# Two fp32 attention layers on one core: 96-row stacks of high and low halves replaced by plain fp32 matmuls on 16-row heads

## What is computed

```
x = x + attention0(layernorm(x), ctx)    # weights W + 2 A B (rank 16), biases
x = x + sqrt((n @ cos(..))**2 + (n @ sin(..))**2),  n = layernorm(x)
x = x + attention1(layernorm(x), ctx)    # q and k are rotated (rope), biases
x = x + quantised feed-forward(layernorm(x)), 256 -> 1024 -> 256
```

## Time and profile before

| | |
|---|---|
| three runs | 2496.88, 2500.81, 2504.37 us; median 2500.81 |
| profiled execution, first to last instruction | 2491.9 us |
| first attention: first to last exponential | 110.6 to 843.6 us |
| second attention: first to last exponential | 1079.7 to 2083.9 us |
| busy over the span: PE, DVE, ACT, POOL | 78%, 70%, 53%, 32% |

### The profile page before, as it was taken

One profiled execution on the slowest core, in us unless ns is written; L12 is line 12 of the kernel. 1 busy time (PEld: TensorE's weight loads), 2 busy tenths in 40 slices (PEclk: granted clock), 3 DMA queues, 4 the chain that ended last, 5 costly groups with the idle time before them and its releaser, 6 DMA issues. The chain is left out here.

```text
span 2491.9 us, 47293 instructions
## 1 busy us (share of the span) xinstructions
PE 1955.9 (78%) x14240; PEld 1576.1 (63%) x14240; DVE 1747.3 (70%) x3674; ACT 1316.8 (53%) x2381; POOL 797.0 (32%) x866
## 2 busy tenths in 40 slices
PE   1689999999999679277788777887777775786687
PEld 0567777777777467255666666666666663665676
DVE  6567778877877378465667767767666665676788
ACT  0255666656655378144444444444444443786676
POOL 3012222222222200423333333333333332221787
PEclk9899999999999689578888888888888877898899
DMA  5576887888878100356665656666666661356565
GB/s 164 107 157 145 169 172 162 166 169 166 170 161 165 53 3 0 76 104 122 123 120 116 117 109 116 119 112 118 111 118 122 121 118 54 135 220 252 196 242 186
DMA packets 259781, 333.54 MB, mean 134 GB/s; under 512 B 29152, under 2 KB 237184, under 8 KB 251520
## 3 DMA queue, kind: packets, MB, share of 16 engines
q1 hardware_dynamic: 233088, 277.00, 49.4%
q0 software_dynamic: 26624, 55.67, 9.6%
HBM read 185.70 MB, written 144.70 MB: 133 GB/s over the span
## 5 line engine op out<-in xcount | busy, mean ns | idle before, releaser
L610 DVE TENSOR_REDUCE L_negm<-L_s_bank 128x2 f32<-128x512 f32 x1024 | 684.4, 684 | 363.2 <-PE L_s_bank L418 360.7
L475 ACT ACTIVATE L_prob<-L_t_bank 128x512 f32<-128x512 f32 x1024 | 598.9, 598 | 631.8 <-PE L_t_bank L429 625.7
L418 PE MATMUL L_s_bank<-L_kst,L_qst 96*128 96x256 f32 x2048 | 526.1, 343 | 236.5 <-DMA L_kst<-k_scratch 176.7
L418 PEld LDWEIGHTS L_s_bank<-L_kst,L_qst 96*128 96x128 f32 x2048 | 355.4, 216 | 363.0 <-issue 142.0
L429 PE MATMUL L_t_bank<-L_qst,L_kst 98*128 98x256 f32 x2048 | 460.6, 311 | 18.3 <-ACT L_prob L475 15.2
L429 PEld LDWEIGHTS L_t_bank<-L_qst,L_kst 98*128 98x128 f32 x2048 | 361.7, 217 | 33.3 <-ACT L_prob L475 30.0
L339 PE MATMUL L_o_bank<-L_prob,L_vext 128*32 128x256 f32 x4096 | 301.1, 415 | 2.7 <-ACT L_prob L475 2.7
L1289 PE MATMUL G_acc<-G_w_out,G_hhl 128*128 128x256 f32 x1024 | 140.4, 291 | 59.4 <-DVE G_hhl L1259 59.1
L259 POOL DMA_DIRECT2D L_den<-o_scratch x64 | 35.5, 554 | 452.2 <-DMA o_scratch<-L_osb 452.2
L1289 PEld LDWEIGHTS G_acc<-G_w_out,G_hhl 128*128 128x128 f32 x1024 | 127.9, 192 | 72.1 <-DVE G_hhl L1259 37.5
L339 PEld LDWEIGHTS L_o_bank<-L_prob,L_vext 128*32 128x32 f32 x4096 | 112.5, 115 | 92.6 <-issue 18.8
(11 more groups left out here) (172 smaller groups left out, 3257.2 us busy)
## 6 DMA issues: line engine op xcount, KB each, us to landing
L_qst<-q_scratch SPq DMA_DIRECT2D x384, 128.0 KB, 5.0
L_kst<-k_scratch SPq DMA_DIRECT2D x384, 128.0 KB, 6.4
q_scratch<-L_qhl SPq DMA_DIRECT2D x64, 512.0 KB, 3.0
k_scratch<-L_khl SPq DMA_DIRECT2D x64, 512.0 KB, 3.2
o_scratch<-L_osb POOLq DMA_DIRECT2D x128, 256.0 KB, 4.8
hidden_scratch<-G_hid SPq DMA_DIRECT2D x32, 1024.0 KB, 3.9
G_hid<-hidden_scratch SPq DMA_DIRECT2D x32, 1024.0 KB, 7.4
L_ctx_in<-in_ctx SPq DMA_DIRECT2D x64, 256.0 KB, 3.2
```

The lines of the kernel that those rows point to most:

```text
L418: mm = pe.matmul(s_bank[k % 2][:, j, :], qst[1 - q][0:96, h, P * qt:P * (qt + 1)], kst[1 - q][0:96, h, :], start=True, stop=True)
L475: act.activation(prob[g % 2][:, k % 2, 2 * (k // 2 % 2):2 * (k // 2 % 2) + 2, :], t_bank[k % 2][:, :, :], ACT.Exp, scale=HD ** -0.5).then_ ...
L610: dve.tensor_reduce(negm[:, t, 2 * pair:2 * pair + 2, qt], s_bank[k % 2][:, :, :], AX.X, ALU.max, negate=True).then_inc(sem["dve_s"], 1)
```

## The change

It touches `attention`, `start` and the constants; the two feed-forward layers stay. A row of the changed kernel names that kernel's own lines (there the scores are L307, the transposed scores L324).

- No halves. A projection is 4 plain fp32 matmuls. Layer 1 has two more weights, `qr` and `kr`, whose output is the rotated half, so that the shuffle and its multiplication go; POOL multiplies both parts with cos and sin at once (1024 elements a partition) and adds them (`rotate`), one q and one k a step.
- Heads lie where the projection puts them, 16 features in each 32-row strip of the array (`qs`, `ks`; the odd heads are copied to the strips' first rows by four transfers each, `odd_heads`). A score matmul contracts 16 rows, a transposed one 17; the 17th holds ones in `ks` and the negated maxima in `qs`. In a slot they are issued in turn, score and transposed score, in strips two apart.
- The weighted sums of a step are two blocks of 16 matmuls (`weighted`) and leave PSUM in one copy `eo` to `osb`. `den` is filled by SP from `osb`, `rden` goes straight to `rin`, two plain fp32 matmuls with `bsel` spread it (L413), VectorE multiplies. The odd heads' results are moved by four transfers (`merge`).
- ctx is transposed once and stored (`c_dram`), layer 1 reads it back. The bias of v goes into that of the output. Normalising x moves from ScalarE to POOL.
- All small transfers stand in SP's queue; POOL issues none. The loop over sequences is unrolled. `drive` makes steps -2 to 33.

```diff
-        qst = [sb(f"qst{j}", [98, H, S], F32R) for j in range(2)]
-        kst = [sb(f"kst{j}", [98, H, S], F32R) for j in range(2)]
-        prob = [sb(f"prob{j}", [P, NT, 4, S]) for j in range(2)]
-        vext = [sb(f"vext{j}", [P, NT, H, SLOT]) for j in range(2)]
-        whl = {n: sb(f"w{n}", [P, 2, KT, D], F32R) for n in "qkvo"}
-        ctx_in = sb("ctx_in", [P, NT, D])
+        NP = 4 if rope else 2
+        qs = [sb(f"qs{j}", [P, 2 * KT, S]) for j in range(3)]
+        ks = [sb(f"ks{j}", [P, 2 * KT, S]) for j in range(3)]
+        prob = [sb(f"prob{j}", [P, NT, 4, KT, S]) for j in range(2)]
...
-        yhl = xT
-        negm = sb("negm", [P, 2, HT, NT])
-        mhl = sb("mhl", [P, 2, 2, HT * NT], F32R)
-        mT = sb("mT", [2 * HT * NT, 2, P], F32R)
+        xT = sb("xT", [P, KT, S])
...
+        bvc = sb("bvc", [P, KT])
+        bvx = sb("bvx", [P, KT, P])
         bo = sb("bo", [P, D])
...
-            cos, sin = sb("cos", [P, S]), sb("sin", [P, S])
-            rr = sb("rr", [P, KT, S])
-        s_bank = [ps(f"s_bank{j}", [P, 2, S]) for j in range(2)]
...
+        t_bank = [ps(f"t_bank{j}", [P, KT, S]) for j in range(2)]
+        eo = ps("eo", [P, 2, KT, S])
+        m0, m1 = ps("m0", [P, KT, S]), ps("m1", [P, KT, S])
...
-        def drive(eng, step):
-
-            for i in range(-2, 5):
-                step(i, i % 2)
-            with eng.Fori(2, (B - 4) // 2) as r:
-                step(2 * r + 1, 1)
-                step(2 * r + 2, 0)
-            for i in range(B - 3, B + 3):
-                step(i, i % 2)
-
...
+        def drive(step):
+            for i in range(-2, B + 2):
+                step(i, i + 2 < B, 0 <= i + 1 < B, 0 <= i < B, 0 <= i - 1 < B, 0 <= i - 2)
...
-            def stack(dst, dram, order, t, done):
-                for c, part in enumerate(order):
-                    sp.dma_start(dst[HD * c:HD * (c + 1), HT * t:HT * (t + 1), :].bitcast(F32),
-                                 dram[part, t].rearrange("(h d) q -> d h q", d=HD)).then_inc(done, 16)
...
+            def odd_heads(buf, done):
+                for g in range(4):
+                    sp.dma_start(buf[32 * g:32 * g + HD, 2:4, :], buf[32 * g + HD:32 * g + 2 * HD, 0:2, :]).then_inc(done, 16)
+
+            def maxima(n, c):
+                sp.wait_ge(sem["dve_mT"], 2 * n + c + 1)
+                sp.dma_start(qs[n % 3][16:P:32, 2 * c:2 * c + 2, :], mT[c][:, :]).then_inc(sem[f"m_load{c}"], 16)
...
+                if d_on:
+                    sp.wait_ge(sem["act_eo"], i)
+                    after(sp, sem["dve_rd"], i - 1)
+                    for c in range(2):
+                        sp.dma_start(den[64 * c:64 * (c + 1), :], osb[(i - 1) % 2][HD - HD * c:P:32, c, :, :]).then_inc(sem["den_load"], 16)
                 if a_on:
...
+                    sp.wait_ge(k_ready, i + 3)
+                    odd_heads(ks[(i + 2) % 3], sem["odd_k"])
+                if d_on:
+                    sp.wait_ge(sem["den_load"], 32 * i)
+                    after(sp, sem["merge"], 64 * (i - 1))
+                    for g in range(4):
+                        sp.dma_start(osb[(i - 1) % 2][32 * g + HD:32 * g + 2 * HD, 0, :, :],
+                                     osb[(i - 1) % 2][32 * g + HD:32 * g + 2 * HD, 1, :, :]).then_inc(sem["merge"], 16)
+                if a_on:
+                    sp.wait_ge(q_ready, i + 3)
+                    odd_heads(qs[(i + 2) % 3], sem["odd_q"])
+                if d_on:
+                    sp.wait_ge(sem["dve_rd"], i)
+                    after(sp, sem["pe_r"], i - 1)
+                    sp.dma_start(rin[:, :], rden[:, :]).then_inc(sem["r_load"], 16)
                 if b_on:
-                    m_rows(i + 1, 1 - q, 0)
+                    maxima(i + 1, 0)
                 if a_on:
...
+                    sp.wait_ge(sem["odd_k"], 64 * (i + 3))
+                    after(sp, sem["ones"], 16 * (i + 2))
+                    sp.dma_start(ks[(i + 2) % 3][16:P:32, 0:2, :], ones[:, :, :]).then_inc(sem["ones"], 16)
+                    sp.wait_ge(sem["odd_q"], 64 * (i + 3))
...
+            def rotate(n, dst, parts, full, free, done, base):
+                pool.wait_ge(full, n + 1)
+                pool.tensor_tensor(parts[:, :, :, :], parts[:, :, :, :], cs[:, :, :].unsqueeze(2).to_broadcast([P, 2, KT, S]),
+                                   ALU.mult).then_inc(sem["pool_rope"], 1)
+                pool.wait_ge(sem["pool_rope"], base + 1)
+                pool.tensor_tensor(dst[:, 0:2, :], parts[:, 0, :, :], parts[:, 1, :, :], ALU.add).then_inc(done, 1)
...
-            def project(dst, wt, act):
-
+            def project(dst, weight, act):
                 for f in range(KT):
-                    group = [(k, cw, ca) for cw, ca in ((0, 0), (0, 1), (1, 0)) for k in range(KT)]
-                    for j, (k, cw, ca) in enumerate(group):
-                        mm = pe.matmul(dst[:, f, :], wt[:, cw, k, P * f:P * (f + 1)], act[:, ca, k, :],
-                                       start=j == 0, stop=j == len(group) - 1)
+                    for k in range(KT):
+                        mm = pe.matmul(dst[:, f, :], weight[:, k, P * f:P * (f + 1)], act[:, k, :], start=k == 0, stop=k == KT - 1)
                 return mm
...
+            def scores(n, k):
+                c, g, qt = k // 8, (k % 8 // 2 + 2) % 4, k % 2
+                if k == 0:
+                    pe.wait_ge(q_ready, n + 1)
...
+                after(pe, sem["dve_s"], 16 * n + k - 1)
+                rows = slice(32 * g, 32 * g + HD)
+                for t in range(KT):
+                    mm = pe.matmul(s_bank[k % 2][:, t, :], qs[n % 3][rows, 2 * c + t, P * qt:P * (qt + 1)], ks[n % 3][rows, 2 * c + t, :],
+                                   start=True, stop=True)
+                    if t == KT - 1:
+                        mm.then_inc(sem["pe_s"], 1)
+                    yield
...
+                after(pe, sem["act_p"], 16 * n + k - 1)
+                rows = slice(32 * g, 32 * g + HD + 1)
+                for t in range(KT):
+                    mm = pe.matmul(t_bank[k % 2][:, t, :], ks[n % 3][rows, 2 * c + t, P * kt:P * (kt + 1)], qs[n % 3][rows, 2 * c + t, :],
+                                   start=True, stop=True)
+                    if t == KT - 1:
+                        mm.then_inc(sem["pe_t"], 1)
+                    yield
...
+                        if a_on and not rope:
+                            pe.wait_ge(sem["ctx_load"], 16 * (n + 1))
+                            after(pe, sem["act_v"], n)
+                            after(pe, sem["dve_y"], i - 1)
...
+                    if k == xT_at and a_on:
+                        pe.wait_ge(sem["pool_xn"], n + 1)
+                        after(pe, sem["dve_mT"], 2 * i + 2)
+                        after(pe, sem["act_k"] if rope else sem["act_q"], n)
                         transposes(m0, xn).then_inc(sem["pe_xT"], 1)
...
+                    if k == o_at and e_on:
+                        pe.wait_ge(sem["dve_y"], i - 1)
+                        pe.wait_ge(sem["act_xT"], min(n + 1, B))
+                        after(pe, sem["dve_mT"], min(2 * i + 2, 2 * B))
+                        after(pe, sem["dve_x"], i - 2)
+                        project_rows(m0, yT, wt["o"]).then_inc(sem["pe_o"], 1)
+                    if k == q_at and a_on:
+                        pe.wait_ge(sem["act_xT"], n + 1)
+                        after(pe, sem["dve_x"], i - 1)
+                        mm = project(m0, wt["q"], xT)
...
+                            after(pe, sem["act_v"], n)
+                            after(pe, sem["dve_y"], i - 1)
+                            mm = project(m1, wt["qr"], xT)
+                        mm.then_inc(sem["pe_q"], 1)
+                    if k == k_at and a_on:
+                        if rope:
+                            pe.wait_ge(sem["ctx_load"], 16 * (n + 1))
+                            pe.wait_ge(sem["act_q"], n + 1)
+                            project(m0, wt["k"], cT[n % 2])
+                            project(m1, wt["kr"], cT[n % 2]).then_inc(sem["pe_k"], 1)
+                        else:
+                            pe.wait_ge(sem["act_cT"], n + 1)
+                            project(m1, wt["k"], cT[0]).then_inc(sem["pe_k"], 1)
+                    if k == v_at and a_on:
+                        pe.wait_ge(sem["act_k"], n + 1)
+                        project_rows(m1, cT[n % len(cT)], wt["v"]).then_inc(sem["pe_v"], 1)
...
+                            pe.wait_ge(sem["act_k"] if rope else sem["act_q"], n + 1)
+                        after(pe, sem["dve_x"], i - 1)
+                        maxima(i + 1, 0)
+                    if k == mT_at and c_on:
+                        weighted(i, 0)
+                    if k == 13 and d_on:
+                        pe.wait_ge(sem["r_load"], 16 * i)
+                        pe.wait_ge(sem["act_v"], min(n + 1, B))
...
+                            mm = pe.matmul(m1[:, t, :], bsel[:, t, :], rin[:, :], start=True, stop=True)
```

(20 more changed lines are left out.)

666 lines of the change are left out of this document (246 added, 420 removed).

## The result

The changed kernel takes 3596.03 us (median of 4 runs, 3591.68 to 3601.81) where the kernel before took 2498.85 on the same chip: 1.441 times, 95% interval 1.4366 to 1.4454. The forecast was 3565 us. The profiled execution spans 3591.4 us, 1099.5 more than before.

A forecast was written before the change was run, and what follows sets the result against it. TensorE's work and waits were taken as the bound; work, turns, waits and low clock gave steps of 34.2 and 54.0 us, +360 and +723 less 18, so 3565 us. Its range was 3350 to 3800, with 3030 to 4000 for 8 in 10.

The forecast's parts named there:

- A plain fp32 record: Matmuls of 256 columns: 0.22 us a record at the full clock, two records or 0.44 us a matmul.
- Pairs side by side: Score and transposed score in two row strips run together: 14.1 us a step, against 28.2 one after the other.
- TensorE's work: Per step at full clock: 27.1 us first attention, 30.2 second, plus 2.0 and 2.1 us for turns between strips and array.
- slots k and k+1 use the same two strips: Scores: neighbouring slots share strips, an argument against four strips at once, which would take 7 us a step.
- "faster" rival: Wait for stacks counts and strips overlap more than in pairs; 2126 us with four strips at once; chance 0.03.
- The price of strips: Scores: by the skill's 3.07 times for four strips, two would give 1.5 times and 18 us; not taken.
- Waits of the first attention: Output projection waits 1.4 us for the copy of xT, score banks cost 0.5; 1.9 us a step.
- Waits of the second: Five a step: output projection 1.5, q 1.8, k 1.7, v 3.0, rin 5.0 us; sum 13.0 us.
- The clock: Few-row scores, and pauses in the second attention, run partly at 1.2 GHz: 3.2 us a step first attention, 8.7 second.
- The sum: Steps of 34.2 and 54.0 us, times 32 sequences: +360 and +723, less 18 for the weight split; span 3557 us.
- serial strips: Rival: row strips do not overlap, 14.1 us more a step; 3960 to 5,100 us, 4,600 in the middle; chance 0.15.
- the high clock: Rival: clock stays high in both attentions, steps of 31.0 and 45.3 us, 3185 us; chance 0.20.

The follow-up runs named there:

- e1_rows: Stand-alone kernel of plain fp32 matmuls, stretches of differing rows and strips, each between 128-row stretches; 0.216 us a record at full clock, one at a time.
- e11_rows_up: Stand-alone fp32 matmul kernel, most kinds now behind 16-row stretches at low clock, three behind 128 rows; windows of 20 to 44 us kept the low level.
- e5_rows32: Changed kernel with scores and transposed scores over all 32 rows of a strip, six buffers zeroed each layer, values not the reference's; 3422.6 us.
- e6_one_strip: Changed kernel with the score of a slot in the same row strip as its transposed score; 4461.9 us.
- e3: Kernel before with its score matmuls reading the stacks of 96 and 98 rows as plain fp32; 3375.5 us.
- e4: Kernel before with plain fp32 score matmuls reading only the first 16 rows of the stacks; 5230.1 us.
- e8: Changed kernel with the load of rin moved ahead of the odd heads of k in SP's queue, both layers; 3577.6 us.
- e10: Changed kernel with scores over all 32 rows of a strip and the rin load ahead in the second attention only; 3338.5 us.

## Why the prediction was right, step by step

- **Bound.** Right: TensorE's work and its waits set the step; VectorE and ScalarE are under 40%.
- **A plain fp32 record** is 0.216 us at the full clock (e1_rows, with 64 and 96 rows alike; 0.22 taken) and 0.42 at the low one (e1_rows and e11_rows_up, with 16, 32 and 64 rows alike). Right, and with it the reading of the rank-16 product as 1.2 GHz.
- **Pairs side by side**: right, and fully.
- **TensorE's work** at the full clock was put too high: 27.1 + 2.0 = 29.1 and 30.2 + 2.1 = 32.3 us against 25.1 and 30.0 by the estimate from busy time and PEclk. The step that failed is "slots k and k+1 use the same two strips". That holds for even k only; slots 2j+1 and 2j+2 have four, and two of them take the time of one. There are five such places in a step of the first attention and four in one of the second, at 4 x 0.216 = 0.86 us each 4.3 and 3.4 us at most. So that condition of the "faster" rival was true in places, but it is far too small to carry the rival.
- **The price of strips.** Where the Trainium skill, TensorE: Matmul & The Clock Gate, Part 3, was weighed (3.07 times for four row strips), the measurement is 0.216 / 0.054 = 4.0 times and decides against it here.
- **Waits of the first attention**: 1.9 us forecast, (1185.0 - 1083.8) / 31.94 = 3.2 measured. Missing were 0.3 us for `rin` and 1.0 us ahead of the transposes of x, which has no releaser in the profile; in the code they wait for their bank until VectorE has copied the turned maxima out of it, and in the step looked at VectorE ends this copy (L514) at 740.20 and the transposes start at 740.30.
- **Waits of the second**: 13.0 forecast, (1681.9 - 1371.7) / 31.94 = 9.7 measured over all steps. Each time that it occurs: `rin` 3.5 against 5.0, v on the copy of k 2.6 against 3.0, q 1.5 against 1.8, output projection 1.25 against 1.5, k 0.6 against 1.7, and the same 1.0 of the transposes, not foreseen. The places were right, the sizes a little high; k's was three times too high. In that of `rin` two errors cancel in part. SP's queue and the wait, in one step:

```profile
2403.32 2.48 SPq L163 DMA_DIRECT2D L_ks<-L_ks  x4
...
2410.96 0.61 SPq L202 DMA_DIRECT2D L_rin<-L_rden  x1
...
2412.84 0.79 PE L413 MATMUL L_m<-L_rin,bsel 16*128 16x256 f32 x1 [3.00 <-DMA L_rin<-L_rden]
```

The twelve transfers took SP 2410.96 - 2403.32 = 7.6 us, 0.64 each, not 5.4. From the start of POOL's rotation of k at 2399.60 to the arrival of `rin` it is 13.2 us, not 11.5. TensorE's own work meanwhile took 10.3 us, not 6.5, because part of it ran at the low clock, and hid more of the chain.
- **The clock.** The mechanism, few rows at 1.2 GHz though busy, was right and is shown twice. Its size is the term that failed most: 3.2 us a step were taken in the first attention and 8.7 in the second, where the estimate from busy time and PEclk gives 8.8 and 12.9. e5_rows32 bears it out: there it gives 29.8 x 0.14 = 4.2 us for the first attention, 4.6 less, and the step fell by 4.05.
- **The sum.** 34.2 against 37.1 (+93 us over the layer), 54.0 against 52.7 (-43), the parts outside the attentions -30 us against -18. These leave the span 34 us over the 3557 forecast. Within a step larger errors cancel: in the first attention work -4.0, waits +1.3, clock +5.6 us; in the second work -2.3, waits -3.3, clock +4.2. The main mechanisms were right, but that the total came within 1% is in part luck. The 9 us that the prediction and the section on the time before put between span and time are too many: the profiled execution after took 3593.19 us with a span of 3591.4.
- **What was to be seen**: pairs 0.21 us apart, PEclk 0.74 and 0.70, the two waits in each step of the second attention (3.5 us for `rin` where about 5 stood): all there.

The rivals: serial strips measured 4462 us (e6_one_strip) where 4600 stood for the middle. No run had the high clock throughout; e5_rows32 at 3423 is two fifths of the way to its 3185. By the estimates above that price was itself too high, as the two steps lose 8.8 and 12.9 us to the clock and not 3.2 and 8.7; how much of it other waits would take back was not measured.

## What to carry to other kernels

Replacing a split into halves by plain fp32 was no saving here, where the halves filled the array's rows: 96 rows in one record of 0.127 us did the work of two records with 16 rows, of 0.216 us each. Price a row strip by what shares the array with it, and look in PEclk for stretches in which TensorE is busy and slow: two strips of 16 rows ran at half the clock, and in the kernel before going from 96 rows to 16 with the same records made the time 1.55 times as long (e3, e4). Before you call a forecast right because its total is, compare each term: here the low clock cost over twice what was taken in the first attention and TensorE's work was less by most of that. In a shared transfer queue a move has two ends: look at what will stand behind the moved wait (e8), and check that the pause has gone and not moved (e10).

## What the runs showed of the hardware

- Rows matter to the clock, not to the price in cycles: TensorE 100% busy was at 1.2 GHz in the windows with 16, 2 x 16, 2 x 17, 3 x 16 and 32 rows, though each of these stretches began behind 128 rows at 2.4 GHz. By the Trainium skill, TensorE: Matmul & The Clock Gate, Part 1, activity releases the throttle; these traces agree only where many rows work (96 rows and four strips of 32 came up from 1.2 GHz, e11_rows_up).
- Three kinds kept the level that they found: 4 x 16, 2 x 32 and 64 rows ran at 2.4 GHz behind 128 rows and at 1.2 GHz behind 16.
- Four row strips, and four column strips, are four times one matmul at a time: 0.054 and 0.053 against 0.216 us a record of 256 columns at the full clock; at the low clock 30.6 / 292 = 0.105 us with four strips of 16 rows against 0.42 with one.
- A short on-chip transfer took SP 0.64 us to issue in a row of twelve, and the load behind them landed 1.9 us after its own issue began (2410.96 to 2412.84).
